# Routing weights spread by transfers through DRAM instead of by eight products, and transposed two chunks sooner

## The reference

```python
x = x + 0.5 * ffn0(layernorm(x))     # changed, called A here
x = x + attn0(layernorm(x))
x = x + 0.5 * ffn0(layernorm(x))     # changed, called B here
...                                  # three more blocks, not touched

def ffn0(x):                         # 16 experts of width 64, two chosen per token
    scores = softmax(xf @ gate_w.T)
    # + gate_b, the best two of four groups of experts, in them the best two experts
    combine = (one_hot(idx, E) * weights[..., None]).sum(1)     # [tokens, 16]
    h = silu(einsum('td,edi->tei', xf, We1) + be1) * (einsum('td,edi->tei', xf, We3) + be3)
    yo = einsum('tei,eid->ted', h, We2) + be2
    y = einsum('te,ted->td', combine, yo)
    z = silu(xf @ ws1 + bs1) * (xf @ ws3 + bs3) @ ws2 + bs2      # the shared expert
    return y + z
```

## Time and profile before

| | us |
|---|---|
| Median of 3 runs (lowest, highest) | 3396.52 (3387.16, 3408.16) |
| Span of the profiled execution | 3381.5 |
| Stage A in it, about | 14 to 442 |
| Stage B in it, about | 1357 to 1784 |

### The profile page before, as it was taken

The page is one execution under the profiler, slowest core; times in us unless marked ns, Lnnn a source line. Parts: engine busy times, 40 slices in busy tenths (PEclk is TensorE's granted clock), DMA queues, the critical chain, the costliest instruction groups (busy, mean ns, idle before and its releaser), DMA issues. The chain is left out here.

```text
span 3381.5 us, 46658 instructions
## 1 busy us (share of the span) xinstructions
PE 2992.5 (88%) x16194; PEld 1802.3 (53%) x16194; DVE 2505.1 (74%) x6050; ACT 1760.5 (52%) x2680; POOL 906.3 (27%) x885
## 2 busy tenths in 40 slices
PE   7999969999999998899995689899799999989863
PEld 5666623444444433666663456566566666656432
DVE  6878768888888871778875698967467778797765
ACT  3444406777777766344434456455344555555544
POOL 2111022121111100111101345556323333343333
PEclk9999968999999986899996589889899999999965
DMA  2000022122122110100000000000000000000000
GB/s 76 1 1 1 1 93 90 59 92 83 65 92 83 66 48 5 51 1 1 1 1 0 1 7 20 13 19 26 32 13 13 13 7 13 13 7 26 7 7 25
DMA packets 33698, 99.03 MB, mean 29 GB/s; under 512 B 4184, under 2 KB 4792, under 8 KB 29240
## 3 DMA queue, kind: packets, MB, share of 16 engines
q1 hardware_dynamic: 31288, 91.85, 7.5%
q10 hardware_dynamic: 2176, 4.19, 0.3%
HBM read 53.56 MB, written 42.47 MB: 28 GB/s over the span
## 5 line engine op out<-in xcount | busy, mean ns | idle before, releaser
L698 DVE TENSOR_REDUCE att_mx<-att_pair 128x2 f32<-128x1024 f32 x512 | 617.3, 1220 | 132.5 <-PE att_pair L947 132.3
L873 ACT ACTIVATE att_pt<-att_pair 128x1024 f32<-128x1024 f32 x512 | 523.0, 1025 | 241.3 <-PE att_pair L957 238.4
L969 PE MATMUL att_o<-att_pt,att_vx 128*32 128x256 f32 x4096 | 339.9, 418 | 9.9 <-ACT att_oT L879 5.1
L947 PE MATMUL att_pair<-att_k,att_q 24*128 24x512 f32 x1024 | 274.2, 539 | 48.2 <-DMA att_k<-att_spread_k 14.2
L957 PE MATMUL att_pair<-att_q,att_k 26*128 26x512 f32 x1024 | 268.0, 525 | 0.1
L957 PEld LDWEIGHTS att_pair<-att_q,att_k 26*128 26x128 f32 x1024 | 99.5, 193 | 199.0 <-issue 169.1
L449 ACT ACTIVATE ffnA_h<-ffnA_up,b 128x512 f32<-128x512 f32 x144 | 99.1, 688 | 189.4 <-PE ffnA_up L105 185.7
L449 ACT ACTIVATE ffnB_h<-ffnB_up,b 128x512 f32<-128x512 f32 x144 | 99.1, 689 | 188.4 <-PE ffnB_up L105 182.5
L947 PEld LDWEIGHTS att_pair<-att_k,att_q 24*128 24x128 f32 x1024 | 101.0, 196 | 134.4 <-ACT att_pt L873 86.9
L969 PEld LDWEIGHTS att_o<-att_pt,att_vx 128*32 128x32 f32 x4096 | 92.1, 112 | 144.6 <-issue 125.3
L1888 ACT ACTIVATE att1k_sq<-att1k_k 128x512 f32<-128x512 f32 x128 | 76.2, 595 | 162.6 <-PE att1k_k L105 162.5
(11 more groups left out here) (543 smaller groups left out, 7972.7 us busy)
## 6 DMA issues: line engine op xcount, KB each, us to landing
att_q<-att_spread_q SPq DMA_DIRECT2D x16, 1024.0 KB, 5.0
att_k<-att_spread_k SPq DMA_DIRECT2D x16, 1024.0 KB, 4.8
att_spread_q<-att_qhi SPq DMA_DIRECT2D x32, 256.0 KB, 2.5
att_spread_k<-att_khi SPq DMA_DIRECT2D x32, 256.0 KB, 3.3
context<-att1k_ctx SPq DMA_DIRECT2D x16, 512.0 KB, 2.6
att1q_cin<-context SPq DMA_DIRECT2D x16, 512.0 KB, 3.3
X<-L_attn_x ACTq DMA_DIRECT2D x8, 512.0 KB, 7.9
att_spread_q<-att_qlo SPq DMA_DIRECT2D x16, 256.0 KB, 2.5
```

Of the source, the lines that this page charges most:

```text
L698: v.tensor_reduce(top[b % 2][:, t, h:h + 2], pair("s", k)[:, :].rearrange("p (h n) -> p h n", h=2), AX, ALU.max, negate=True).then_inc(mx, 1)
L873: a.activation(pt[k % 8][:, :, :].rearrange("p h n -> p (h n)"), pair("t", k)[:, :], ACT.Exp, scale=scale).then_inc(p_, 1)
L947: last = pe.matmul(pair("s", k)[:, (j - j0) * 512:(j - j0 + 1) * 512], qb[b % 3][r, u, t * P:(t + 1) * P], kb[b % 3][r, u, :], start=True, ...
L969: last = pe.matmul(obank[j * BLOCK:(j + 1) * BLOCK, cols], vxb[b % 3][:, t, 4 * u + j, :], pt[(2 * g + j // 2) % 8][:, j % 2, cols], start ...
```

## The change

The eight `spread` products are gone. The weights are transposed into a bank of their own (`comb`, the former `cw`) at step 6 instead of behind step 8, with a third copy of them, unrounded, in rows 32 to 47. ACT copies those 16 rows to SBUF (`plain`), SP writes them to a DRAM tensor `kept` (32 KB), waits until they have landed, and issues eight loads that read the rows back, each over 64 partitions: two experts' rows for two chunks, 256 KB a load, 2 MB a group. `weighed` multiplies by that tile in SBUF, and waits for the semaphore of its two loads. The exponential moves from behind the first SiLU of a pass to behind the last SiLU of the pass before. In B the weight tiles use memory that a later stage's tensors take, which is why a tensor set is freed earlier.

```diff
         def weighed(i, c):
             n, e = E9(i, c), E8(i, c)
-            v.wait_ge(S.cw, e + 1)
+            v.wait_ge(S.cw[c // 2], 32 * (i + 1))
...
-            v.tensor_tensor(hc[e % 4][:, :], cw_bank(i, c)[:, :], h3[n % HELD][:, :], ALU.mult).then_inc(S.hc, 1)
+            v.tensor_tensor(hc[e % 4][:, :], weight(c), h3[n % HELD][:, :], ALU.mult).then_inc(S.hc, 1)
...
         def combined(i):          # ACT
             a.wait_ge(S.cT, i + 1)
+            if i:
+                a.wait_ge(S.kept, 16 * i)
+            a.activation(plain[32:48, :], combb[32:48, :], ACT.Copy).then_inc(S.plain, 1)
...
-            a.activation(combT[i % 2][0:32, :], misc[0:32, :], ACT.Copy).then_inc(S.ct, 1)
+            a.activation(combT[i % 2][0:32, :], combb[0:32, :], ACT.Copy).then_inc(S.ct, 1)
...
-                if c == 0 and i < groups:
-                    exps(i)
-            if i < groups:
-                combined(i)
+                if c == 7 and i < groups:
+                    combined(i)
+                if c == 8 and i + 1 < groups:
+                    exps(i + 1)
...
         def combined(i):          # PE
             pe.wait_ge(S.comb, i + 1)
...
-                last = pe.transpose(misc[0:32, t * P:(t + 1) * P], pairb[i % 2][:, t, :].bitcast(F32), ident[:, :])
+                last = pe.transpose(combb[0:48, t * P:(t + 1) * P], pairb[i % 2][:, t, :].bitcast(F32), ident[:, :])
...
-                if i and c < CHUNKS - 1:
-                    spread(i - 1, c)
...
+                if c == 6 and i < groups:
+                    combined(i)
                 if c == 7 and i + 1 < groups:
                     gate(i + 1)
-            if i < groups:
-                combined(i)
...
+    def sync(sp):
+        if prefetch:
+            prefetch(sp)
+        halves = kept.rearrange("(c e) n -> e c n", e=2)
+        for i in range(groups):
+            sp.wait_ge(S.plain, i + 1)
+            if i:
+                for landed in S.cw:
+                    sp.wait_ge(landed, 32 * i)
+            sp.dma_start(kept, plain[32:48, :]).then_inc(S.kept, 16)
+            sp.wait_ge(S.kept, 16 * (i + 1))
+            for part, landed in enumerate(S.cw):
+                if i:
+                    sp.wait_ge(S.hc, E8(i - 1, 2 * part + 2))
+                for e in range(2):
+                    sp.dma_start(weights[part][INTER * e:INTER * (e + 1), :].rearrange("p (c n) -> p c n", c=2),
+                                 halves[e, 2 * part:2 * part + 2, :].unsqueeze(0).to_broadcast([INTER, 2, GROUP])).then_inc(landed, 16)
```

More of the change, by code:

```diff
@@ L207, in __init__, with ffn0 @@
         (self.var, self.root, self.xn, self.xT, self.xh, self.xl, self.lt, self.sh, self.ex, self.comb, self.cT, self.ct, self.up1,
-         self.up3, self.sil, self.gl, self.cw, self.hc, self.dn, self.y, self.yo, self.add) = signals(
-            nc, ctx, name, "var root xn xT xh xl lt sh ex comb cT ct up1 up3 sil gl cw hc dn y yo add")
+         self.up3, self.sil, self.gl, self.plain, self.kept, self.hc, self.dn, self.y, self.yo, self.add) = signals(
+            nc, ctx, name, "var root xn xT xh xl lt sh ex comb cT ct up1 up3 sil gl plain kept hc dn y yo add")
+        self.cw = signals(nc, ctx, name, "cw0 cw1 cw2 cw3")
         self.st, self.stated = Steps(nc, ctx, name + "_chain"), Steps(nc, ctx, name + "_stats")
 HELD = CHUNKS + 3
-def ffn0(nc, S, name, X, W, K, groups, arrived=None, prefetch=None):
+def ffn0(nc, S, name, X, W, K, groups, arrived=None, prefetch=None, spare=None):
     mem = Memory(nc, name)
@@ L230, in ffn0 @@
     combT = mem.ring("combT", 2, [P, GROUP], F32R)
+    plain = mem.sb("plain", [3 * EXPERTS, GROUP])
+    weights = [w[:, :] for w in spare or mem.ring("weights", 4, [P, 2 * GROUP])]
+    weight = lambda c: weights[c // 2][:, c % 2 * GROUP:c % 2 * GROUP + GROUP]
+    kept = nc.dram_tensor(name + "_weights", [EXPERTS, GROUP], F32, kind="Internal").ap()
     routing = [{**{k: mem.sb(f"r{i}_" + k, [P, TILES, n])[:, :, :] for k, n in ROUTING},
                 **{k: mem.sb(f"c{i}_" + k, [P, TILES])[:, :] for k in ("mx", "sum", "best")}} for i in range(2)]
-    pairb = mem.ring("pairb", 2, [P, TILES, 32], F32R)
-    misc, ltb, cwb, acc = mem.ps("misc"), mem.ps("lt"), mem.ps("cw"), mem.ps("acc")
+    pairb = mem.ring("pairb", 2, [P, TILES, 3 * EXPERTS], F32R)
+    misc, ltb, combb, acc = mem.ps("misc"), mem.ps("lt"), mem.ps("comb"), mem.ps("acc")
     up = [mem.ps(f"up{i}") for i in range(4)]
@@ L238, in ffn0 @@
     xg = lambda i: X[:, i, :, :]
-    cw_bank = lambda i, c: up[c % 4] if i == groups - 1 and c else cwb
     def chunk_of(e):
@@ L437, in scalar @@
         high(0)
+        exps(0)
         for i in range(groups + 1):
@@ L477, in combined @@
             pe.wait_ge(S.comb, i + 1)
[L478 to L481 removed]
+            if i:
+                pe.wait_ge(S.ct, i)
             for t in range(TILES):
[L483 removed]
+                last = pe.transpose(combb[0:48, t * P:(t + 1) * P], pairb[i % 2][:, t, :].bitcast(F32), ident[:, :])
             last.then_inc(S.cT, 1)
@@ L487, in back @@
             pe.wait_ge(S.y, i + 1)
-            pe.wait_ge(S.ct, min(i + 2, groups))
-            if i == groups - 1 and i:
+            pe.wait_ge(S.xl, min(i + 3, groups))
+            if i:
                 pe.wait_ge(S.add, i)
             turn_back(pe, misc, yT[i % 2], ident).then_inc(S.yo, 1)
-        def spread(i, c):
-            e = E8(i, c)
-            if c == 0:
-                pe.wait_ge(S.ct, i + 1)
-            if i == groups - 1 and c:
-                pe.wait_ge(S.gl, CHUNKS * groups)
-                if c >= 5:
-                    pe.wait_ge(S.hc, e - 3)
-            elif e:
-                pe.wait_ge(S.hc, e)
-            pe.matmul(cw_bank(i, c)[:, :], K["spread"][:, c, :], combT[i % 2][:, :], start=True, stop=True).then_inc(S.cw, 1)
         def down(n):
@@ L2458, in macaron @@
             W = ffn0_tensors(right)
-            A = attn0_tensors(right)
+            attending = layer0.enter_context(ExitStack())
+            A = attn0_tensors(lambda name, shape: attending.enter_context(nc.sbuf_tensor(name, shape, F32, side="right")))
             with stage(nc) as s:
@@ L2465, in macaron @@
                 attn0(nc, s, "att0", X, A, K, groups)
+            attending.close()
             V = ffn1_tensors(keep)
@@ L2470, in macaron @@
             with stage(nc) as s:
-                ffn0(nc, Ffn0Signals(nc, s, "ffnB"), "ffnB", X, W, K, groups, prefetch=loads1(d, R, T, landed))
+                ffn0(nc, Ffn0Signals(nc, s, "ffnB"), "ffnB", X, W, K, groups, prefetch=loads1(d, R, T, landed),
+                     spare=[w[:, :].bitcast(F32) for w in T["wk"] + T["gk"]])
         with stage(nc) as s:
```

30 lines of the change are left out of this document (13 added, 17 removed).

## The result

| | before | after |
|---|---|---|
| Median us (lowest, highest), 20 runs each | 3388.3 (3354.69, 3408.16) | 3414.36 (3386.04, 3442.09) |
| Span of the profiled execution | 3381.5 | 3384.2 |
| Stage A, start of the first statistics to start of the last residual sum | 426.2 | 442.7 |
| Stage B, likewise | 425.5 | 441.6 |
| A group of A in its steady part | 25.60 | 25.8 to 27.2 |

What follows compares the result with a forecast made beforehand. PE was taken as the bound, then a loop: landing 8.3, DVE's chain 16.77, 0.05 to PE, 0.1 for POOL, 25.2 us a group against 25.60; about 3 us saved in two stages, median 3393, range 3365 to 3430.

Steps and rivals of the forecast that it cites:

- What bounds the kernel, and where the gain goes: Stage A: PE bounds before; afterwards PE waits 1.4 us at the transposes, leaving 0.4 of the 1.84 us saved a group.
- C: The start of a group's transposes of the routing weights on PE, from which the prediction counts times in us.
- The write: Weights' write to DRAM: 2.01 us to the start of a dependent read, taken from a 256 KB row for 32 KB.
- The pair of loads: First two 256 KB loads of a group: 3.6 us to landing, 3.3 from the 512 KB row plus 0.3 for issue.
- rival 3: Weights land late because 64-partition loads run at half rate: pair 4.7 us, 32 us slower in all, 3428; chance 0.20.
- the main case: Rival 1, no gain left: lap 24.6 to 25.8 us, kernel 3374 to 3412 us; chance 0.66.
- The landing: First pair of weights lands at C + 8.3, 0.5 us later than DVE needs; the first product waits for it.
- the sign that the prediction named: A DVE wait of 1.5 us or more ahead of the first product would show rival 3.
- The start and the tail: Stage A: first C at 44.1; after the last C, 8.3, 0.75 and 6.9 us to the last product, at 437.45.
- POOL: Normalization on POOL meets DVE's products that read SBUF twice: 0.1 us charged a group.
- Rival 4: POOL shuts DVE out: 0.79 us for each of the first two products, 1.5 more a lap, 3438; chance 0.06.
- The case that the prediction gave 0.08: Rival 2, PE stays the bound: 1.84 us gained a lap, 59 us in two stages, 3337; chance 0.08.

Runs made afterwards that it cites:

- x1: Changed kernel with only the first group's weights written and loaded, later groups multiplying by those; lap 24.91 us, stages A and B 420.1 and 420.7 us.
- x6: Changed kernel with only the transposes one step later, at the end of step 7; lap 24.3 to 25.7 us, stages 421.7 and 421.2 us.
- x5: Changed kernel with products by the weights one step later on DVE and transposes at the end of step 7; lap 23.47 us, ratio to before 0.9877.
- x9: Changed kernel with each pair of loads replaced by one 512 KB load over 128 partitions, first expert's rows only; lap 24.93 us, stages 423.8 and 423.9 us.
- x2: Changed kernel with eight spare PE products ahead of PE's wait at the transposes; mean lap 26.10 us, stages 441.0 and 442.5 us.
- x7: Changed kernel with the first pair of loads split into four of 128 KB over 64 partitions; lap 24.93 us, stages 424.0 and 422.1 us.
- x3: Changed kernel with each product by the weights one step later on DVE; lap 24.87 us, ratio to before 0.9994.
- x4: Kernel before with transposes, copies and exponential moved, `spread` products kept, no transfers; lap 27.10 us, stages 453.9 and 451.4 us.
- x10: Changed kernel with transposes and copies put back behind step 8, exponential left where the change has it; lap 30.6 us, stages 508.4 and 507.4 us.

## Why the prediction was wrong

It named the right loop and put the result on the wrong side of zero. By its own steps:

- **What bounds the kernel, and where the gain goes**: right. PE stopped being the bound, and the lap is the landing of the weights, DVE's chain, and PE's transposes. DVE's part was 16.68 us for 16.77, the sum came at C + 7.24 for 7.15, the copy ended at C + 2.66 for 2.6, the jump from chain to transposes took 0.05. x1, x6 and x5 confirm both ends: without the landing the lap is 24.91, without PE's stop the wait moves to DVE, and without both it is PE's own 23.47.
- **The write**: 1.56 us to the next load's issue, not 2.01. The row used was for 256 KB, this write has 32 KB; the bound from below should have been lower. It gave back 0.45 us a lap.
- **The pair of loads is the step that failed.** "Its bytes are those of the 512 KB row" was taken for 3.6 us. It measured 4.99 in the lap shown and 4.79 in the tail, 1.2 to 1.4 more, close to the 4.7 of rival 3; 0.3 of that is the second load's issue, 0.64 where 0.33 was taken. x9 shows that one load over all 128 partitions does take 3.57 here, and with it the stages are 2.4 and 1.6 us shorter than before, the 1.7 that the prediction gave: this one term turned a small gain into the loss. By the runs the pair ran at 235 GB/s where the whole width gave 369, 0.64 of it and not the half that the rival assumed, and the second load added to that. The Trainium skill (SBUF - State Buffer, "Can I just issue two DMAs to hit both halves?") says that two transfers to two halves gain only 6% over one. The trace agrees in kind: issued 0.64 us apart, the two ran together at two thirds of the full width's rate. The prediction had that reason in hand and weighed it at 0.20, because no row showed a transfer to 64 partitions. The absence of a row is no evidence for the better case; the rival deserved about as much as the main case.
- **The landing** became C + 9.2 for 8.3, so the steady lap is 25.96 for 25.2. Over the 15 laps that is 11.4 us. A wait of 1.5 us or more was to mark rival 3; it is 1.28, since the write gave back 0.45. So the sign that the prediction named would have missed the rival that came.
- **A term that was missing: PE's clock.** The prediction let PE idle 1.4 us a lap and asked nothing more. It idles 2.3 to 2.5, because the lap is 0.8 longer and PE's own lap 0.3 shorter, and after that the clock falls in 8 of the 28 laps behind the first of either stage:

```profile
200.62 0.62 PE L487 MATMUL ffnA_comb<-ident,ffnA_pairb 128*48 128x128 f32 x4 [2.27 <-DVE ffnA_pairb L354]
...
201.31 0.63 PE L104 MATMUL ffnA_up<-ffnA_xl,w_hi 128*128 128x512 f32 x1
201.74 0.63 PE L105 MATMUL ffnA_up<-ffnA_xh,w_lo 128*128 128x512 f32 x1
...
227.84 0.40 PE L104 MATMUL ffnA_up<-ffnA_xl,w_hi 128*128 128x512 f32 x1
228.08 0.39 PE L105 MATMUL ffnA_up<-ffnA_xh,w_lo 128*128 128x512 f32 x1
```

  These are PE's rows after: behind an idle time of 2.27 us the products stand 0.43 apart, in the next lap 0.24. Slow laps are 26.5 to 27.2 long, since a slower step 7 and 8 make the exponential late. The 15 laps of A took 393.54 us, where the prediction had 15 x 25.2 - 0.6 = 377.4: 11.4 of these 16.1 us are the steady lap's, 4.7 what some laps have above it: 3.8 in the four at 0.94, of which x2 gave back 2.0, and 0.7 in the first.
- **The start and the tail.** The first transposes stand at 42.59, not 44.1, 1.5 us gained. In the tail the last product came 18.6 behind C where 15.95 was worked out: the parts of the weights land 2.2 us apart, not the "about a microsecond" of the text, and DVE has no chain there to cover it. That is 2.7 us. The sum closes: -1.5 + 16.1 = 14.6 at the last C (436.13 against 421.5), and 14.6 + 2.7 = 17.3 at the last product (454.73 against 437.45), so that the gain of 1.7 us a stage became a loss of 15.6.
- **POOL**: the charge on DVE was right in size; what the meeting costs shows on the other engine. The changed products, POOL's normalization before, and the same after, in stage A (duration ns min/median/max):

```profile
L372 DVE TENSOR_TENSOR ffnA_hc<-ffnA_weights,ffnA_h x128: 668/684/801, 53.0 to 452.8; 128x512 f32<-128x512 f32 x128
```

```profile
L154 POOL TENSOR_SCALAR ffnA_xn<-X,ffnA_mv,ffnA_rstd x64: 787/796/818, 18.1 to 385.0; 128x128 f32<-128x128 f32 x64
```

```profile
L154 POOL TENSOR_SCALAR ffnA_xn<-X,ffnA_mv,ffnA_rstd x64: 783/800/1368, 17.2 to 396.9; 128x128 f32<-128x128 f32 x64
```

```profile
236.32 3.90 POOL L154 TENSOR_SCALAR ffnA_xn<-X,ffnA_mv,ffnA_rstd 128x128 f32<-128x128 f32 x4
```

  The longest of DVE's 128 products took 0.12 us more than the median. But in the lap shown above, where POOL begins at 236.32 and the product at 236.38, POOL's four instructions take 3.90 us instead of the 3.15 of the earlier trace rows, and the longest single one of the stage 1.37 instead of at most 0.82. The Trainium skill (SBUF - State Buffer, "SBUF: two separate sides") says that of such a pair the one that starts first has the shared port for its whole instruction and the other fully blocks. The trace agrees that one of the two blocks, with POOL as the loser: 1.37 - 0.80 = 0.57 us, most of a product's 0.69; that the first to start wins it does not show. It costs the kernel nothing, for POOL has time to spare: 68.36 of 417 us busy. Rival 4 had the right mechanism on the wrong engine.
- **The range and the line of 1%.** The median after lies inside the range, and the change within 1%. But the interval excludes no change, and the forecast of a small gain was wrong. What the range covered was rival 3 as the prediction priced it, at 32 us in all, and about that is what came, in part by luck: the clock and the tail added to it, and the write gave back 0.45 us in each lap, 14 in the kernel.

The case that the prediction gave 0.08, PE as the bound, was one step away: x5 reaches it with the same transfers, because it lets both the transposes and the first product wait less, by asking for each a step later.

## What to carry to other kernels

Where a wait is moved forward on one engine and its answer comes back through another, write down the loop from the wait to itself: its length is the new lap, and shortening anything outside it gains nothing. Both ends of such a loop can be set by when they are asked for: one step later for the transposes and one for the products turned a loss of 0.9% into a gain of 1.2%. A transfer should be priced by its partitions as well as its bytes, and the first part that someone waits for should be small.

## What the runs showed of the hardware

- Two loads of 256 KB over 64 partitions each, issued 0.6 us apart, had landed 4.8 to 5.0 us behind the first's issue in the places shown, and ran at 235 GB/s with the DMA engines all busy; one load of 512 KB over 128 partitions had landed in 3.6 (3.9 in stage B's tail) and ran at 369. A load of 128 KB over 64 partitions lands in 2.9.
- Eight loads whose source starts with a dimension of two entries and that fill 128 partitions hold SP for 30.67 us instead of 5.12, and move 49 GB/s at a DMA share of 0.13.
- A write of 32 KB from SBUF to DRAM releases the dependent issue on its queue after 1.56 us.
- A POOL instruction that reads SBUF while DVE multiplies two tiles in SBUF takes up to 1.37 us instead of 0.80; DVE's product loses 0.12 at most in stage A.
- Behind the first lap of a stage, PE's granted clock fell in 9 of the 20 laps that follow 2.1 to 2.5 us of idle time at the transposes (after, x7 and x9; in after to the lower level from 202 to 204), and in none of the 148 that follow 1.2 to 1.9 us of it (the same kernels, x1, x3 and x4). In x10, where PE stands 4.70 us for a bank in each lap, the clock averaged 0.88 to 0.89 in all of them. One lap of x6 in stage B fell without such idle time at the transposes; its cause is open.
- The attention stage, which is the same work in both kernels, took 882.55 us at a clock of 0.93 in one profiled execution and 913.79 at 0.88 in another. One span against another says little here.
